# Decoder kernel: layers as straight code, and the probability transposes moved behind the value projection

## What is computed

```
for i in range(6):
    x = attn_layer(shift_tokens(x), Wqkv[i], q_scale[i], k_scale[i], Wo[i]) + x
    x = ffn_layer(shift_tokens(x), ln_g[i], ln_b[i], W1[i], b1[i], W2[i], b2[i]) + x

attn_layer:  q, k, v = split(x @ Wqkv)             # 16 heads of 64
             q, k = l2norm(q) * qs, l2norm(k) * ksc, both rotated
             sim  = 8 * q @ k.T over a window of 32, masked
             out  = softmax(sim) @ v, then @ Wo
ffn_layer:   layernorm, a * gelu(gate) with W1 (2 x 341), then @ W2
```

## Time and profile before

| | |
|---|---|
| time, median of 3 runs (lowest to highest) | 4241.02 us (4237.38 to 4242.67) |
| profiled execution: its own time | 4239.87 us |
| its span, first to last instruction | 4238.0 us |
| busy share of the span: PE / DVE / ACT / POOL | 93% / 87% / 84% / 80% |
| two small attentions and what comes ahead of layer 0 | 0 to 714 us |
| layers 0 to 4 (L1670 at 714.0, 1301.9, 1892.0, 2481.7, 3072.9, 3658.3) | 588, 590, 590, 591, 585 us |
| layer 5 and the end | 3658 to 4238 us |
| one turn of the inner loop (8 steps) late in layer 5 | 31.70 us |

### The profile page before, as it was taken

How to read it: one execution, slowest core, us unless ns; L and a number is a source line. 1 busy time by engine, 2 the same in 40 slices (tenths; PEclk the granted TensorE clock), 3 DMA queues, 4 the chain that set the end, 5 groups by cost and what they waited for, 6 DMA issues and landing times. The chain is left out here.

```text
span 4238.0 us, 138593 instructions
## 1 busy us (share of the span) xinstructions
PE 3921.8 (93%) x49504; PEld 3104.8 (73%) x49504; DVE 3702.8 (87%) x8896; ACT 3553.0 (84%) x11595; POOL 3381.8 (80%) x2461
## 2 busy tenths in 40 slices
PE   7998885999989999989999989999899999999998
PEld 5665664777777777767777777777677777777776
DVE  7998887999988999979999889999789998899996
ACT  6988995999967999949999769999589998699995
POOL 4554446999968999959999779999599998799993
PEclk9999997999999999999999999999999999999999
DMA  3000000000000000010000000000100000000001
GB/s 84 0 0 1 0 0 16 4 2 0 0 21 22 5 0 0 2 40 4 2 0 0 15 28 5 0 0 1 40 5 3 0 0 10 17 6 0 0 0 36
DMA packets 81153, 39.23 MB, mean 9 GB/s; under 512 B 60084, under 2 KB 73266, under 8 KB 80946
## 3 DMA queue, kind: packets, MB, share of 16 engines
q1 hardware_dynamic: 80946, 36.56, 3.3%
HBM read 21.92 MB, written 2.10 MB: 6 GB/s over the span
## 5 line engine op out<-in xcount | busy, mean ns | idle before, releaser
L1215 POOL TENSOR_TENSOR rnorm<-norm2g,neg_half 128x16 f32<-128x16 f32 x384 | 1116.2, 2907 | 187.7 <-DVE norm2g L1513 178.6
L1053 ACT ACTIVATE pair<-pair,top 128x128 f32<-128x128 f32 x3072 | 1056.5, 345 | 37.9 <-DVE top L1520 24.1
L1207 POOL TENSOR_TENSOR rotated<-by_cos,by_sin 128x512 f32<-128x512 f32 x768 | 987.6, 1286 | 76.0 <-DVE by_sin L1496 73.9
L1227 POOL TENSOR_TENSOR rotated<-rotated,rnorm 128x512 f32<-128x512 f32 x768 | 786.5, 1047 | 0.5
L699 PE MATMUL bank<-wqkv_high,xt_high 128*128 128x512 f32 (+1 forms) x1536 | 652.9, 425 | 30.0 <-issue 19.5
L1053 ACT ACTIVATION_READ_ACCUMULATOR pair<-pair,top 128x1 f32 x3072 | 650.8, 212 | 0.0
L1488 DVE TENSOR_TENSOR by_cos<-bank,rot_cos 128x512 f32<-128x512 f32 x768 | 530.0, 690 | 102.7 <-PE bank L699 95.8
L1064 ACT ACTIVATE vout<-bank 128x512 f32<-128x512 f32 (+1 forms) x810 | 466.1, 575 | 148.6 <-PE bank L772 131.7
L772 PE MATMUL bank<-prob_t,vout 128*32 128x128 f32 x12288 | 494.8, 279 | 101.6 <-ACT prob_t L1070 60.2
L1044 ACT ACTIVATE squares<-bank 128x512 f32<-128x512 f32 x768 | 459.1, 598 | 135.9 <-DVE by_sin L1496 115.2
L1538 DVE TENSOR_TENSOR prob<-pair,rsum 128x512 f32<-128x512 f32 x768 | 530.8, 691 | 40.8
(11 more groups left out here) (142 smaller groups left out, 8453.9 us busy)
## 6 DMA issues: line engine op xcount, KB each, us to landing
wqkv_sb<-in_L_ffn_Wqkv_dram SPq DMA_DIRECT2D x36, 256.0 KB, 4.1
ctx_all<-y SPq DMA_DIRECT2D x48, 128.0 KB
ctx_all<-y SPq DMA_DIRECT2D x48, 127.0 KB
wo_sb<-in_L_ffn_Wo_dram SPq DMA_DIRECT2D x48, 64.0 KB, 2.0
out_dram<-y SPq DMA_DIRECT2D x8, 256.0 KB, 3.5
w_sb<-in_L_ffn_W_dram SPq DMA_DIRECT2D x6, 341.0 KB, 3.1
w_sb<-in_L_ffn_W_dram SPq DMA_DIRECT2D x12, 64.0 KB
cst<-in_constants_dram SPq DMA_DIRECT2D x1, 582.0 KB, 3.8
```

Source lines behind the costliest of these rows:

```text
L1053: last = nc.scalar.activation(at, at, ACT.Exp, bias=top[jl % 2][:, h:h + 1], accum_out=psum_raw[jl % 2][:, h:h + 1])
L1207: nc.gpsimd.tensor_tensor(rotated[j % 4][:, :, :, :], by_cos[j % 2][:, :, :, :], by_sin[j % 2][:, :, :, :], ALU.add).then_inc(c_rot, 1)
L1215: nc.gpsimd.tensor_tensor(rnorm[slot][:, :, :].rearrange("t g n -> t (g n)"), norm2g[slot][:, :, :].rearrange("t g n -> t (g n)"), neg_hal ...
L1227: nc.gpsimd.tensor_tensor(at, at, rnorm[slot][:, i, :].unsqueeze(2).to_broadcast([P, 2 * HG, DH]), ALU.mult).then_inc(c_unit, 1)
```

## The change

Two edits. `layers` no longer makes a loop: each of the six layers is written out on each engine, with the layer number as a constant. Inner loops (L423, L431) stay. And in `win_products`, on TensorE alone, `win_values` comes ahead of `win_turn_probs`.

```diff
-        def layers(eng, first, body):
+        def layers(first, body):
 
             first()
-            with eng.Fori(0, DEPTH - 1) as layer:
-                body(layer, False)
-            body(DEPTH - 1, True)
+            for layer in range(DEPTH):
+                body(layer, layer == DEPTH - 1)
...
             def win_products(layer, it, j):
                 win_project(layer, it, j)
+                win_values(layer, it, j)
                 win_turn_probs(layer, it, j)
-                win_values(layer, it, j)
                 win_mask(layer, it, j)
...
-            layers(pe, first, body)
+            layers(first, body)
```

More of the change, by code:

```diff
@@ L1158, in body @@
                     win_copy_next(layer + 1, 0, 3)
-            layers(act, first, body)
+            layers(first, body)
         @block.gpsimd
@@ L1325, in _ @@
             set_sines(0)
-            layers(pool, first, body)
+            layers(first, body)
         @block.vector
@@ L1750, in _ @@
             dve.wait_ge(s_tiny_set, 2)
-            layers(dve, first, body)
+            layers(first, body)
             dve.wait_ge(s_y_done, (DEPTH + 1) * NQ)
```

## The result

The changed kernel takes 4247.26 us (median of 20 runs, 4244.64 to 4249.55) against 4240.78 us before (20 runs, 4237.38 to 4243.04): a ratio of 1.0015, 95% interval 1.0008 to 1.0022, or **+6.5 us**. The interval leaves out 1, so the loss is real, but it is under the 0.2% that the prediction called distinguishable, and far less than the +25 us forecast. Both halves of the change work, and they nearly cancel. Most of what follows is about their sizes.

The account below looks back on a forecast made before the run. A step is the longer of ScalarE's and TensorE's paths from L772 to `prob_t`, ScalarE's before the change. Profiled 4239.9 + 54.5 (swap) - 28.6 (layer loop) = 4265.8, forecast 4266 us, range 4246 to 4285 (chance 0.62).

Parts of the forecast that it names:

- A plain step gets 0.08 us longer: Inner-loop steps without input transpose, 91 per layer: `prob_t` starts 1.78 us behind the projection, not 1.70, as transposes end later.
- The mid-turn step: Step in mid-turn where an input transpose delays TensorE, 15 per layer: `prob_t` loses 0.12 us (1.78 against 1.66).
- the step behind the branch: Step after the inner loop's branch, 15 per layer: ScalarE is late there (1.93 us), 1.78 is early enough, no loss.
- TensorE's weight load at L772 idle for 0.5 us: Ahead of the first value product, waiting for `prob_t`: idle 0.27 us should become 0.27 + 0.08 + 0.16, about 0.5.
- Idle time ahead of `prob_t` that the transposes ended: Sign on ScalarE: in seven of eight steps the `prob_t` copy would show idle time that TensorE's transposes ended.
- The layer loop: Four turn-backs of the loop over layers: straight code gives back 6.94 + 7.01 + 6.94 + 7.71 = 28.6 us.
- Register instructions are hidden already: Written-out steps of layer 5 have the same spacing as those in the loops, so nothing was booked.
- Rival 1: Transposes are in time after all, so only the layer loop counts: 4211 us, faster; chance 0.15.
- rival 2: TensorE sets the pace, so 0.16 us per step come back, 116 us: 4095 us; chance 0.05.
- Rival 3: A TensorE pause of 0.20 us ahead of the moved transposes, costing 186 us in all: 4397 us; chance 0.08.
- Rival 4: Straight code does not remove the stall at layer edges, which has another cause: 4294 us; chance 0.06.
- rival 5: One of six inner loops, now placed elsewhere in a longer program, turns back dearly, costing 60 us: 4326 us; chance 0.04.

Follow-up runs that it names:

- unroll_only: Changed kernel with TensorE's old order in `win_products` (transposes ahead of `win_values`), so straight layers alone: 4214.05 us, ratio 0.9932 against the kernel before.
- swap_only: Kernel before, its loop over layers kept, with `win_values` ahead of the transposes: 4281.5 us, ratio 1.0092 against the kernel before.
- all_straight: Straight layers in the old order, with the attention's inner loop (L423) written out too: 4192.43 us, ratio 0.9889 against the kernel before.
- early_: ScalarE's first exponential ahead of `vout`, VectorE's maximum ahead of division: straight layers, old order 4211.83 us; changed kernel 4231.36; old order with inner loop written out 4195.16.
- two_ahead: Changed kernel with two of the three 256-wide value products ahead of the transposes, the third behind them: 4213.81 us, ratio 0.9932 against the kernel before.
- behind_mask: Changed kernel with the mask also ahead of the transposes, and the wait for the probabilities ahead of the values: 4523.04 us, ratio 1.0659 against the kernel before.

## Why the prediction was off

- **The mechanism was right.** In plain steps the tie moves from ScalarE's path to TensorE's. The four experiments that shorten one path in each order show it: each shortening pays 40 to 66 us in one order and 6 us or nothing in the other.
- **The step that failed: "A plain step gets 0.08 us longer".** It got 0.05 (3.853 against 3.803 in the mean). Of the missing 0.03, the larger part, 0.02, lies behind `prob_t`: the next L771 starts 0.65 us after it, not 0.67, as the copy is a 0.60 us one. I took the way from `prob_t` to L772 over unchanged, although shows a copy that waited for its transposes at 0.60. The other 0.01 lies ahead: `prob_t` starts 1.77 us behind the projection in the mean (1.76 in the step above), where I took 1.78, and the transposes 1.13, not 1.14 as in the earlier trace rows. On the page the mean `prob_t` fell from 618 to 600 ns:

```profile
L1069 ACT ACTIVATE prob_t<-bank 128x512 f32<-128x512 f32 x768 | 460.8, 600 | 3.9 <-PE bank L757 3.9
```

- **The mid-turn step** (+0.11: 4.42 against 4.31) and **the step behind the branch** (no loss: 4.55 against 4.57 in `unroll_only`) came nearly as predicted. Only 12 steps of a layer stand behind a branch, not 15. Two of the other three lost 0.10 to 0.11 us each.
- **The sum.** In the profiles, attention grew by 37.6 us from `unroll_only` in place of 54.5. Plain steps make 28.6 us of that where I had 43.7 (91 x 0.08 x 6), mid-turn steps 9.5 where I had 10.8. The medians give 33 us. The forecast named 0.08 as its weak term and said that 0.01 is 6.4 us. With 0.05 the term is at the edge of its 0.03 either way, and 4247.26 at the low end of its 4246 to 4285. But loss and gain nearly cancel, so an error of a third in the loss is most of the change.
- **A turn** takes 32.07 to 32.10 us late in layer 5, not 32.30. The prediction's own tests put a turn inside 31.9 to 32.7, so those did not flag it.
- **"TensorE's weight load at L772 idle for 0.5 us"** was wrong: 0.31. The mask started 1.65 us behind the projection, not 1.50. I let it follow the transposes as quickly as the 256-wide product did, 0.36 us behind their start, and it took 0.53. The mask had stood 0.21 us behind the start of the product ahead of it before, too (3962.75 to 3962.96), where 256-wide products follow each other in 0.12. Nobody waited for it, so it cost nothing.
- **"Idle time ahead of `prob_t` that the transposes ended"** was the wrong thing to look for: 3.9 us in the whole span. A wait of 0.06 us vanishes in the overlap of ScalarE's records (0.15 us between read and copy where it was 0.09). It was found by shortening ScalarE's path until the gap showed.
- **The layer loop** was right: 6.9, 7.0, 6.9 and 7.7 us per edge, 28.6 together, and 28.8 measured for straight layers alone. TensorE's stall and the half clock behind it are both gone. One small term was put at nothing: "Register instructions are hidden already". In layers 0 to 4 of the kernel before the step behind the inner branch takes 4.63 us in the mean, in its layer 5 and in `unroll_only` 4.56 to 4.58, some 3 us in all. So 28.8 hits 28.6 in part by luck, as those 3 us and the falls of the clock also move it. The rule of the Trainium skill that the prediction cited ("Runtime: NRT & Kernel Launch", Instruction fetch mechanics), that a taken branch whose target isn't at hand waits for a fetch, agrees with these runs: the 19.5 us of idle time come with the four branches and go with them. That a fetch is what TensorE waits for, no run here shows.
- **Rivals.** Rival 1 (no cost of the swap) and rival 2 fall by `swap_only`. Rival 3's pause ahead of the moved transposes did not come: they start 0.12 us behind the last 256-wide product. Rival 4 falls by `unroll_only`. For rival 5 there is no sign: no inner step grew when the loops changed place.
- **What stays open.** Over the 14 profiled executions, the stretch from W1 to the last L1571 takes 83.4 to 84.3 us in the 37 layers without a fall of the clock, 85.2 to 85.6 in the 29 with one and 87.0 to 87.1 in the four with two. What decides whether the clock falls was not tried. The length of the program alone does not: straight layers alone have four falls, `all_straight` has two. In the `early_` kernels there is one in 15 layers.

## What to carry to other kernels

When an engine hands over its place as the last to arrive, what a step loses is the difference of two paths of nearly equal length. Multiply its error by the number of steps before trusting it, and follow both paths all the way to the next common event, with the durations that the operations have when they wait. Test such a tie by shortening one path in both orders: the one that pays is the bound. And try the parts of a change apart: here one half was worth 0.7% and the other cost 0.8 to 0.9%.

## Not expected

- **A short loop's branch has a price too.** The inner loop's turn-back shows as 0.25 us in one step of eight (4.57 against 4.32), and writing it out gave 21.6 us (4214.05 - 4192.43). The loop turns back 12 times in each of six layers, so 72 x 0.25 = 18 us of that are this step, and 18 us is also what the two ratios give (0.9932 - 0.9889). A layer's turn-back cost 6.9 to 7.7 us each.
- **A change of the kind of product costs TensorE some 0.1 us each time, whatever order it comes in.** The mask (64 x 64) starts 0.20 to 0.21 us behind the start of the instruction ahead of it, be that a 256-wide product (before) or a transpose (changed kernel); only in `two_ahead` it is 0.29. The 256-wide products follow each other in 0.12. Back from the mask to the 128 x 128 transposes in `behind_mask` it is about the same (0.22), and L691 starts 0.20 us behind the last of the 16 small products. So moving the transposes between projection and mask adds no such change, and putting the mask ahead of them, as `behind_mask` does, puts two on the path. Whether the size of the tile or the type makes the difference, no run here separates.
- **The chain of waits does not name the transposes.** Between 3900 and 4030 us the chain of the changed kernel has no piece of L757 at all, although it sets every plain step. The 0.04 us between its end and `prob_t` is covered by ScalarE's records, and the chain follows the instruction ahead on the same engine. One step of it (start, duration, what):

```profile
3951.36 0.60 ACT vout L1063
3951.95 0.50 ACT qk_t L1034
3952.45 1.40 ACT pair L1052 x8
3953.85 0.54 ACT prob_t L1069
```
